# Cross-attention and FP4 feed-forward on one core: a folded value-output matrix made from high and low parts, with its weights loaded in pieces

## The reference

```python
x = x + xattn(layernorm(x), ctx, Wq, Wk, Wv, Wo, bo)     # x: (4, 1024, 256), ctx: (4, 154, 192)
#   16 heads of 64: q = x Wq, k = ctx Wk, v = ctx Wv
#   out = softmax(q k^T / 8) v, heads side by side; out @ Wo + bo
x = x + ffn(layernorm(x), w_gate, w_up, w_down)          # hidden size 704
#   every operand is rounded to FP4 in blocks of 16 with a scale for each block
#   h = silu(xq @ gate^T) * (xq @ up^T); y = hq @ down^T
```

## Time and profile before

| what | value |
|---|---|
| median of 3 runs | 878.01 us (877.73 to 878.34) |
| the profiled execution's own time | 877.47 us |
| its span, first to last instruction | 875.7 us |
| TensorE busy | 833.6 us (95%) |
| VectorE busy | 710.0 us (81%) |
| GpSimd busy | 540.4 us (62%) |
| ScalarE busy | 523.2 us (60%) |
| mean granted TensorE clock | 0.990 of full |
| DMA | 24.30 MB, 28 GB/s |

### The profile page before, as it was taken

The page is one execution under the profiler, slowest core; times in us unless marked ns, Lnnn a source line. Parts: engine busy times, 40 slices in busy tenths (PEclk is TensorE's granted clock), DMA queues, the critical chain, the costliest instruction groups (busy, mean ns, idle before and its releaser), DMA issues.

```text
span 875.7 us, 19198 instructions
## 1 busy us (share of the span) xinstructions
PE 833.6 (95%) x6302; PEld 806.1 (92%) x6302; DVE 710.0 (81%) x2155; ACT 523.2 (60%) x1868; POOL 540.4 (62%) x810
## 2 busy tenths in 40 slices
PE   7876999999999999999999999999999999999986
PEld 6766899999989999999988999999988999999986
DVE  4899788878787888877877888887877888888887
ACT  5554666666665666666665666667656666666531
POOL 4758578765456666664644666665654666676644
PEclk9999999999999999999999999999999999999998
DMA  6310000002010000002010000001100000000000
GB/s 193 101 52 6 9 18 13 26 13 55 14 47 21 13 26 13 20 13 61 8 49 19 13 26 13 25 14 31 38 7 20 13 25 14 13 19 13 7 7 19
DMA packets 20756, 24.30 MB, mean 28 GB/s; under 512 B 2061, under 2 KB 18869, under 8 KB 20661
## 3 DMA queue, kind: packets, MB, share of 16 engines
q1 hardware_dynamic: 19573, 22.04, 8.7%
q10 hardware_dynamic: 1088, 1.05, 0.4%
HBM read 18.89 MB, written 4.19 MB: 26 GB/s over the span
## 4 chain that ended last, share of the span: by engine, by line
PE 78%; DVE 14%; issue 3%; ACT 2%; POOL 2%; DMA 0%; DVEq 0%; ACTq 0%; POOLq 0%
PE ps_g L1331 12%; PE ps_s L1284 10%; PE ps_q L1239 10%; PE ps_t L1296 7%; PE ps_o L1311 7%; PE ps_o L1313 7%; PE ps_o L1312 7%; PE ps_m L1161 3%; PE ps_m L1345 3%; PE ps_m L1347 2%; PE ps_m L1346 2%; PE ps_g L1195 2%; DVE negmax L907 2%; PE ps_g L1184 2%; DVE pT_lo L781 2%
## 5 line engine op out<-in xcount | busy, mean ns | idle before, releaser
L519 POOL TENSOR_TENSOR probs<-probs,rsum 128x308 f32<-128x308 f32 x256 | 180.2, 704 | 226.9 <-DVE rsum L890 226.4
L668 ACT ACTIVATE probs<-ps_s,negmax 128x154 f32<-128x154 f32 x512 | 194.6, 386 | 204.7 <-DVE negmax L907 203.0
L907 DVE TENSOR_REDUCE negmax<-ps_s 128x2 f32<-128x308 f32 x256 | 121.0, 473 | 81.3 <-PE ps_s L1284 80.5
L1311 PE MATMUL ps_o<-B_sb,pT_lo 128*128 128x256 f32 x640 | 180.6, 282 | 0.8 <-DVE x_both L1011 0.5
L1313 PE MATMUL ps_o<-B_sb,pT_hi 128*128 128x256 f32 x640 | 180.5, 282 | 0.0
L1312 PE MATMUL ps_o<-B_sb,pT_hi 128*128 128x256 f32 x640 | 180.1, 281 | 0.0
L781 DVE TENSOR_TENSOR pT_lo<-ps_t,pT_hi 128x256 fp32r<-128x256 f32 (+1 forms) x256 | 122.9, 480 | 31.3 <-ACT pT_hi L595 31.1
L1331 PE MATMUL ps_g<-WGU,xqT_hi 128*128 128x352 f32 x504 | 132.2, 344 | 2.0 <-DVE B_sb L781 1.7
L1296 PE MATMUL ps_t<-ident,probs 128*128 128x128 f32 x640 | 113.5, 275 | 16.6 <-DVE pT_lo L781 14.4
L1311 PEld LDWEIGHTS ps_o<-B_sb,pT_lo 128*128 128x128 f32 x640 | 120.6, 188 | 1.3 <-issue 0.7
L1313 PEld LDWEIGHTS ps_o<-B_sb,pT_hi 128*128 128x128 f32 x640 | 121.2, 189 | 0.0
(11 more groups left out here) (236 smaller groups left out, 2193.6 us busy)
## 6 DMA issues: line engine op xcount, KB each, us to landing
xa<-in_x_dram SPq DMA_DIRECT2D x33, 128.0 KB, 2.2
xr<-in_x_dram SPq DMA_DIRECT2D x32, 128.0 KB, 2.0
out_dram<-y_xn SPq DMA_DIRECT2D x30, 128.0 KB, 1.7
W_sb<-in_L_xattn_Wk_dram SPq DMA_DIRECT2D x3, 768.0 KB, 5.8
W_sb<-in_L_xattn_Wv_dram SPq DMA_DIRECT2D x2, 768.0 KB, 5.2
probs<-in_L_xattn_Wq_dram ACTq DMA_DIRECT2D x4, 256.0 KB, 5.3
Wo_sb<-in_L_xattn_Wo_dram SPq DMA_DIRECT2D x1, 1024.0 KB, 6.1
W_sb<-in_L_xattn_Wv_dram SPq DMA_DIRECT2D x2, 384.0 KB, 3.4
```

The lines of the kernel that those rows point to most:

```text
L519: pool.tensor_tensor(unit, unit, rsum[:, 2 * u:2 * u + 2].unsqueeze(2) .to_broadcast([P, 2, M]), ALU.mult).then_inc(norm_p, 1)
L668: ins = act.activation(probs[:, h, 0:M], ps_s[k % 2][:, s * M:(s + 1) * M], ACT.Exp, bias=negmax[:, h:h + 1], accum_out=sums[:, h:h + 1])
L907: dve.tensor_reduce(negmax[:, 2 * k:2 * k + 2], ps_s[k % 2][:, 0:UM].rearrange("p (h m) -> p h m", h=2), AX_X, ALU.max, negate=True).then_ ...
L1311: pe.matmul(ps_o[:, 0:C], lo[:, j, :], w[:, 0:C], start=first, stop=False)
```

## The change

- B's blocks are no longer fp32 products. The V columns of a job are copied into V_sb, a high part by ScalarE (`v_hi_part`) and a low part by GpSimd (`v_lo_part`), 128x256 elements for each job, in the slot in which the job is made, in two buffers that alternate. Wo is held in a high and a low part too, made once in the first four slots of tile 0 (`wo_hi_part` on ScalarE, `wo_lo_part` on GpSimd, 128x512 elements each).
- A whole block is three fp32r products. The block in halves is six products of 64 rows each, which all write the same 128 rows of PSUM. TensorE waits for its own third product before the fourth (`half_mm`).
- For batch 0 Wk and Wv have buffers of their own, in the place of later parts of B_sb, so they are loaded without a wait for K. For the other batches the weights come in four pieces each through the one buffer W_piece, each piece loaded when the product with the last one is done. W_piece lies where the low part of V_sb lies.
- Jobs are moved between slots and banks (`JOBS`). In batches 1 to 3 the four K jobs now all end in the step "k", and A3 and C3 are in the first slot of "settle". In "v" the transposed x goes to ps_q.
- gu has one buffer for the two that it had, and pT's first buffer two blocks for three.

```diff
@@ memory @@
-        W_sb = sb("W_sb", [CH, 2, INNER])
-        Wo_sb = sb("Wo_sb", [P, PAIRS, C])
+        with nc.sbuf_tensor("W_piece", [CH, 2, 2 * P], F32) as W_piece:
+            pass
+        V_sb = [sb(f"V_{n}", [P, 2, 2 * P], F32R) for n in ("lo", "hi")][::-1]
+        Wo_sb = [sb(f"Wo_{n}", [P, PAIRS, C], F32R) for n in ("hi", "lo")]
...
+        with ExitStack() as early:
+            early.enter_context(nc.sbuf_tensor("B_first", [P, 8, 2 * C], F32))
+            Wk_all, Wv_all = (early.enter_context(nc.sbuf_tensor(n, [CH, 2, INNER], F32)) for n in ("Wk_all", "Wv_all"))
+            Wo_raw = early.enter_context(nc.sbuf_tensor("Wo_raw", [P, PAIRS, C], F32))
...
-        gu = sb("gu", [P, 2, QF])
+        gu = sb("gu", [P, QF])
@@ JOBS @@
-                      6: [("C", 2, "0"), ("D", 1, "q"), ("A", 3, "1")], 7: [("C", 3, "0")]},
-            "v": {0: [("V", 0, "0")], 1: [("V", 1, "1")], 3: [("V", 2, "q")], 5: [("V", 3, "q")]},
-            "k": {2: [("K", 0, "q")], 4: [("K", 1, "q")], 7: [("K", 2, "0"), ("A", 0, "1")]},
-            "roll": {0: [("C", 0, "0"), ("D", 0, "1")], 1: [("A", 1, "0"), ("K", 3, "1")], 3: [("C", 1, "q")],
-                     5: [("A", 2, "q")], 6: [("C", 2, "q"), ("D", 1, "0")], 7: [("A", 3, "q"), ("C", 3, "1")]},
-            "settle": {},
+                      6: [("C", 2, "0"), ("D", 1, "q")], 7: [("A", 3, "1"), ("C", 3, "0")]},
+            "v": {0: [("V", 0, "0")], 1: [("V", 1, "1")], 3: [("V", 2, "q")], 7: [("V", 3, "0")]},
+            "k": {2: [("K", 0, "q")], 4: [("K", 1, "q")], 6: [("K", 2, "0")], 7: [("K", 3, "q")]},
+            "roll": {0: [("A", 0, "0"), ("C", 0, "1")], 1: [("D", 0, "1")], 3: [("A", 1, "q")], 5: [("C", 1, "q")],
+                     6: [("A", 2, "q"), ("C", 2, "0")], 7: [("D", 1, "0")]},
+            "settle": {0: [("A", 3, "1"), ("C", 3, "0")]},
...
-            return ps_m if setup else ps_q
+            return ps_m if setup and setup[0] != "v" else ps_q
@@ SyncE, batches 1 to 3 @@
+            def setup_io(b):
+                pair = b * PPB - 1
+                sp.wait_ge(b_mm, B_JOBS * b)
+                load_piece(Wv, 0)
+                residual(pair, 0)
+                store(pair - 2, 0)
+                for i in range(1, 3):
+                    sp.wait_ge(v_mm, KV * b + i)
+                    load_piece(Wv, i)
+                residual(pair, 1)
+                sp.wait_ge(v_mm, KV * b + 3)
+                load_piece(Wv, 3)
+                ahead_io(pair)
+                sp.wait_ge(v_mm, KV * b + 4)
+                load_piece(Wk, 0)
+                store(pair - 2, 1)
+                sp.wait_ge(k_mm, KV * b + 1)
+                load_piece(Wk, 1)
+                residual(pair + 1, 0)
+                for i in range(2, 4):
+                    sp.wait_ge(k_mm, KV * b + i)
+                    load_piece(Wk, i)
...
@@ GpSimd @@
+            def wo_lo_part(i):
+                pool.wait_ge(wo_hi, i + 1)
+                pool.tensor_tensor(Wo_sb[1][:, 2 * i:2 * i + 2, :], Wo_raw[:, 2 * i:2 * i + 2, :],
+                                   Wo_sb[0][:, 2 * i:2 * i + 2, :].bitcast(F32), ALU.subtract).then_inc(wo_lo, 1)
+            def v_lo_part(job, b):
+                pool.wait_ge(vs_hi, job_at(job, b) + 1)
+                pool.tensor_tensor(v_part(job, 1), v_cols(job, VT_rows), v_part(job, 0).bitcast(F32), ALU.subtract)\
+                    .then_inc(vs_lo, 1)
...
             def first(t, setup):
                 for k in range(SLOTS):
                     normalise(t, k)
+                    for job in b_jobs(jobs_at(setup, k)):
+                        v_lo_part(job, 0)
+                    if t == 0 and k < KV:
+                        wo_lo_part(k)
                     if t == 0 and k == 0:
                         rstd(mv1, rs1, nm1, (ln1_v, 9), ln1_p, 8)
                     if raw_at(t, k, 1) is not None:
                         round_chunk(raw_at(t, k, 1))
@@ ScalarE @@
+            def v_hi_part(job, b):
+                kind, i, _ = job
+                act.wait_ge(v_ev, KV * b + (2 * i + 2 if kind == "D" else i + 1))
+                act.wait_ge(k_mm, KV * (b + 1))
+                if some(job_at(job, b) - 1):
+                    act.wait_ge(b_mm, job_at(job, b) - 1)
+                act.activation(v_part(job, 0), v_cols(job, VT_rows), ACT.Copy).then_inc(vs_hi, 1)
@@ VectorE @@
+                if some(Q * n + q):
+                    dve.wait_ge(h_v, Q * n + q)
@@ TensorE @@
-                for u, at, row, rows in pieces:
-                    ins = pe.matmul(ps[row:row + rows, :], VT[:, u, at:at + rows], Wo_sb[:, u, :],
-                                    start=True, stop=True)
+                hi, lo = (v_part(job, part)[:, n, :] for part in range(2))
+                pieces = [(slice(0, P), u if at < 2 else u + 1)]
+                if at == 2:
+                    pieces = [(slice(D, P), u), (slice(0, D), u + 1)]
+                terms = [(v[h], Wo_sb[a][h, w, :]) for h, w in pieces for v, a in ((lo, 0), (hi, 1), (hi, 0))]
+                for i, (v, w) in enumerate(terms):
+                    if i == 3:
+                        ins.then_inc(half_mm, 1)
+                        pe.wait_ge(half_mm, GROUPS * b + block // 5 + 1)
+                    ins = pe.matmul(ps, v, w, start=(i == 0), stop=(i == len(terms) - 1))
...
-                    pe.wait_ge(v_ev, KV * b + (2 * i + 2 if kind == "D" else i + 1))
+                    if b == 0:
+                        pe.wait_ge(wo_lo, 2 * i + 2 if kind == "D" else i + 1)
+                    pe.wait_ge(vs_lo, job_at(job, b) + 1)
```

More of the change, by code:

```diff
@@ L146, in ctx_bank @@
             return (ps_s[0], ps_s[1], ps_g[0], ps_g[0], ps_m)[r][:, (r == 3) * 2 * P:(r == 3) * 2 * P + 2 * P]
-        ld_ctx, ld_rest, ld_w, ld_wo, ld_bo = (sem(n) for n in ("ld_ctx", "ld_rest", "ld_w", "ld_wo", "ld_bo"))
-        ld_wk, ld_wv = sem("ld_wk"), sem("ld_wv")
+        ld_ctx, ld_rest, ld_w, ld_bo = (sem(n) for n in ("ld_ctx", "ld_rest", "ld_w", "ld_bo"))
+        ld_wk, ld_wv, ld_wo = ([sem(f"{n}{i}") for i in range(2)] for n in ("ld_wk", "ld_wv", "ld_wo"))
+        wo_hi, wo_lo = sem("wo_hi"), sem("wo_lo")
+        vs_hi, vs_lo = sem("vs_hi"), sem("vs_lo")
+        half_mm = sem("half_mm")
         ld_wq = [sem(f"ld_wq{i}") for i in range(4)]
@@ L238, in xattn_ffn_kernel, with job_at, v_cols, v_part @@
         B_JOBS = len(B_ORDER)
+        def job_at(job, b):
+            return B_JOBS * b + B_AT[job[:2]]
+        def v_cols(job, rows):
+            kind, i, _ = job
+            v = rows.rearrange("p (g n) -> p g n", n=4 * MP)
+            if kind == "D":
+                return v[:, 2 * i:2 * i + 2, 4 * P:5 * P]
+            a = 0 if kind == "A" else 2 * P
+            return v[:, i, a:a + 2 * P].rearrange("p (g n) -> p g n", n=P)
+        def v_part(job, part):
+            return V_sb[part][:, B_AT[job[:2]] % 2, :].rearrange("p (g n) -> p g n", n=P)
         B_NEED = [1, 3, 4, 5, 6, 8, 9, 10]
@@ L242, in xT_bank, with b_jobs @@
         def xT_bank(setup):
-            return ps_m if setup else ps_q
+            return ps_m if setup and setup[0] != "v" else ps_q
         def jobs_at(setup, k):
-            return JOBS[setup[0]].get(k, []) if setup else []
+            return JOBS[setup[0]].get(k, []) if setup and setup != ("settle", 0) else []
+        def b_jobs(jobs):
+            return [job for job in jobs if job[0] in ("A", "C", "D")]
         def jobs_before(setup, k):
@@ L556, in step @@
                         normalise(t, k - 1)
+                    for job in b_jobs(jobs_at(setup, k)):
+                        v_lo_part(job, setup[1])
                     if raw_at(t, k, 2) is not None and (t, k) != (1, 0):
@@ L680, in first @@
                     exponentials(t, k)
+                    for job in b_jobs(jobs_at(setup, k)):
+                        v_hi_part(job, 0)
                     if k >= 2:
@@ L719, in step @@
                         take_hi(job, setup[1])
+                    for job in b_jobs(jobs_at(setup, k)):
+                        v_hi_part(job, setup[1])
                     if gate and 3 <= k < Q + 3:
```

131 lines of the change are left out of this document (61 added, 70 removed).

## The result

The changed kernel takes 902.98 us (901.27 to 906.59, six runs) against 878.17 (877.71 to 879.13, six runs): a ratio of 1.0286, interval 1.0271 to 1.0301. That is +24.8 us. I had said slower, and +11.4: the direction holds, the size does not, and the time lies above the range. The profiled execution's span is 901.6 us, 25.9 over the 875.7 before, so the profile shows the whole of it.

A forecast was written before the change was run, and what follows sets the result against it. TensorE was taken to bound ordinary and setup tiles, VectorE and what feeds it the first two. 877.5 + 10.7 (first tile, after the second's slack) + 1.2 (three setups) = 889.4; range 878.5 to 898.

The forecast's parts named there:

- slot 3: First tile: GpSimd's Wo low part, chunk 1 and normalise precede D0's low part at 41.85; next largest score 7.5 late.
- the rounds of slots 4 to 7: First tile: each slot becomes one round through the engines, 5.9, 7.35, 6.95 and 7.4 for 4.98, 5.51, 7.51 and 4.30.
- the second tile: VectorE idles 2.1 there and takes up all of it, bringing the first tile's 12.8 down to +10.7.
- the setups: Tiles carrying a setup: +1.1 - 1.9 + 1.0 + 0.2 = +0.4 each, three times +1.2 (bounds -1.5 and +2.5 each).
- Slot 2: First tile: two Wo low parts delay GpSimd's chunk 0, normalise and V low parts; A0 from 34.7, not 26.90.
- The clock: Rival, chance 0.14: in the first tile's slots 2 to 7 longer waits bring half-clock spells, +6, total 895.
- the sign that I had named for it: Granted clock at 0.5 for over 10 us of the first 90 would show that the clock rival holds.
- the products: TensorE's B products in a setup: six jobs 0.9 less, four C jobs 2.0 more, net +1.1 (bounds +0.5 to +1.3).
- the pieces: Setups: each W piece loads only after the one before is used; V1 the tightest, +0.2 (0 to 0.6).
- the change of shape: C jobs on TensorE: changing tile shape in and out takes 0.27, 0.13 each.
- the fourth of the waits that I had as removed: Setups: TensorE's 0.3 wait, a transpose behind a weight's low part, last of four removed waits totalling 1.9.
- K3's wait: Tile after K3 in a setup: the first query product waits for K's low part, +1.0 (0 to 1.5).

The follow-up runs named there:

- e1: The changed kernel with Wo's third and fourth high parts made on ScalarE ahead of the slot's B high parts: 898.77 against 877.82, ratio 1.0247.
- e6: e1 with V's high part ahead of the exponentials on ScalarE and V's low part ahead of the normalise on GpSimd: 888.72 against 879.06, ratio 1.0104.
- e2: The changed kernel with 128 unused TensorE products added where it waits in the first tile: 899.63 against 877.82, ratio 1.0252.
- e12: e6 with V low parts of A0, C0, D0 ahead of FFN chunks, two Wo low parts two slots later, A3 in slot 6: 888.67 against 877.92, ratio 1.0122.
- e8: e6 with 64 added TensorE products ahead of A0 and D0: 889.30 against 879.06, ratio 1.0120.
- e4: The kernel before with only the new order of jobs and V's x transposes in ps_q, B still in fp32: 872.15 against 877.82, ratio 0.9932.

## Why the prediction was wrong in size

**Where the 14 us are.** The forecast was +11.9 over the profiled execution before, the measured growth is +25.9. In the prediction's own terms: slot 3 7.0 more, the rounds of slots 4 to 7 4.6 more, the second tile 5.2 more, and 2.9 less in the setups and the third tile.

**Slot 2: right.** "Now A0 from 34.7": 34.20, behind the chunk, the bias, the normalise and the low part, as in the sum. TensorE's waits there name GpSimd's subtraction, as I said they would. The job pair that I gave 2.3 us took 4.35, at half clock.

**Slot 3: the step that failed.** "GpSimd: Wo low to 36.7, chunk 1 ... D0's low part at 41.85 ... +7.5." I took the Wo low part as ready when GpSimd was. Its input came from ScalarE, behind the B high part of C0. It ended at 41.3, D0 started at 46.46, and the largest score was 14.5 late, 7.0 more than I had. I had written down each engine's queue and GpSimd's work, but of `wo_lo_part` only its duration, not its `wait_ge(wo_hi, i + 1)`. Of the 7.0, 4.6 are D0's late start, and e1 gives 3.3 back by cutting the link. 2.0 are the clock: D0, V2 and four transposes take 46.46 to 50.64, 4.2, where I had 2.2.

**Slots 4 to 7: mis-sized.** The rounds cost +9.9 for +5.3. The form was right: e6 makes the tile 8.3 shorter with the same work, only by putting V's parts ahead of the round. The terms that I listed give 5.6 for slot 4 and 7.3 for slot 5, where I wrote 5.9 and 7.35, and slots 6 and 7 had no working. Nearly all of the miss, 3.9 of 4.6, is in these two, and the largest part of it is the clock; I had priced every job at the full one: the pair of slot 7 takes 4.35 for 2.49, and the last 9 of slot 6's 15 products run at half clock too. With the added products of e2 the two slots are 2.2 and 0.8 shorter. A3's place has no part in it in the order in which it was tried (e12). What else sets slot 7 I have not separated.

**"I let it take up all of that", the second tile's 2.1: wrong.** From the second tile's first largest score to its end it is 27.5 for 24.4, 3.1 longer and not 2.1 shorter. With the clock held up in e2 the tile is 27.59, 0.7 shorter than before, so the clock is a part of this as well; the rest was not tried.

**The clock: rival and forecast were one case.** I gave it +6 as an alternative at 0.14; it came together with the waits, and the sign that I had named for it is there. In the changed order it is worth 3 to 5 of 24.8 (e2). In e6's order e8 gives 0.5 in the tile and nothing in the median. So its price depends on the waits, and it can't be added as a fixed sum. My argument against it was that most of a slot is "a wait for other engines, which no clock lengthens". That holds where what TensorE waits for doesn't itself wait for TensorE. In the changed order it does, through the B high parts; this fits both runs, but was not tried apart.

**The setups: the sum right within its bounds, by luck in part.** +0.4 each predicted, -0.35 measured. What the change has besides the moves costs 1.45 (e4 against the changed kernel) where I had 1.1 for the products and 0.2 for the pieces. The term that was too small is the change of shape, 0.19 and not 0.13: a C job costs 0.56 more than before and not 0.51, the products together 1.3 and not 1.1. The moves gain 1.8 where I had 0.9: the fourth of the waits that I had as removed is still there (0.4, a transpose behind a weight's low part), so more than the named waits went; what, I have not separated. The two misses cancel in part. K3's wait is there, in the place predicted, 0.8 for 1.0:
```profile
PE ps_q L1326 <- DVE K_lo L872: 0.8, 1, 0.8
```
The pieces cost about nothing. The slot that I called the tightest is 0.1 longer, and a piece lands in 2.5:
```profile
W_piece<-in_L_xattn_Wv_dram SPq DMA_DIRECT2D x12, 192.0 KB, 2.5
```
gu in one buffer and the shorter pT cost nothing, as said: an ordinary pair is 45.52 for 45.61. For the copies on ScalarE and GpSimd in the setups the products leave 0.1 to 0.2.

**What the first tile is made of.** From 69.10, one change after the other: 5.2 with the link through ScalarE cut, 8.3 with V's parts ahead of the rounds, 2.2 with GpSimd's new order. The medians bear out the first two and not the third. Each step has its share of the clock in it. That leaves 53.46 for 41.94. Of these 11.5, 0.9 come with the moves (e4), and slot 0 holds 1.5 that are not the order's: the same order had 4.93 there in e12. Slots 2 and 3 together hold 2.7, and GpSimd is full there; slots 5 and 7 hold 5.3 and 3.8, slot 6 gives 1.6 back. How much of that is GpSimd's work, how much rounds and how much clock stays open.

## What to carry to other kernels

Where work is given to an engine that looks free, write down for each new instruction both what stands ahead of it in its queue and where its inputs are made, and follow these to the end: if the path comes back to the engine that waits, its price is paid in every round and not once. Where the trace shows work behind a wait at half clock, as it did here in the kernel before, price the work behind longer waits so too. Moves and arithmetic that come in one change are to be timed apart: here the moves alone gave 0.7%, and the rest of the change, the arithmetic with its copies and loads, took some 3.5% away. The block in halves, the costliest part of it, costs no more than a whole block in fp32 with one more copy of the weights, and that kernel is 1.3% under the kernel before.
